# Second attention of a small vision tower: 68-column block-diagonal weights, dense head rows, sums from a column of ones

## The reference, cut to what matters

```
dist = softmax(mean(x @ Wr + br, axis=1))          # one row of 16 per image
idx = sort(top_k(dist, 4))
Qs, Ks, Vs = the 4 chosen heads of x @ Wq + bq, x @ Wk + bk, x @ Wv + bv    # 64 features each
score = softmax(Qs Ks^T / 8)                       # 17 x 17 per image and head
O = score Vs                                       # 17 x 64 per image and head
return h + O.reshape(b, s, 256) @ Wo + bo
```

## Time and profile before

| | us |
|---|---|
| median of three runs | 391.5 |
| profiled execution | 390.81 |
| its span | 389.0 |
| TensorE busy | 314.6 (81%) |
| VectorE busy | 257.0 (66%) |
| ScalarE busy | 203.2 (52%) |
| GpSimd busy | 169.3 (44%) |
| TensorE's mean granted clock | 0.851 of full speed |

### The profile page before, as it was taken

How to read it: one execution, slowest core, us unless ns; L and a number is a source line. 1 busy time by engine, 2 the same in 40 slices (tenths; PEclk the granted TensorE clock), 3 DMA queues, 4 the chain that set the end, 5 groups by cost and what they waited for, 6 DMA issues and landing times.

```text
span 389.0 us, 14942 instructions
## 1 busy us (share of the span) xinstructions
PE 314.6 (81%) x6334; PEld 253.9 (65%) x6334; DVE 257.0 (66%) x546; ACT 203.2 (52%) x463; POOL 169.3 (44%) x193
## 2 busy tenths in 40 slices
PE   1999999888977888785897468998889698585787
PEld 0897768535855565554795258888789687483366
DVE  2355446455578888887696776797878678462365
ACT  1023323465877777742488037777777566352320
POOL 4755000004266666642055074576657656563200
PEclk9999999999975555555698559999999999679989
DMA  7997810003500000000000068999998899824714
GB/s 206 373 424 246 248 79 0 0 0 127 199 4 5 4 3 6 3 5 3 3 2 1 0 211 266 287 289 288 258 284 272 241 286 276 249 51 97 229 54 178
DMA packets 52275, 55.97 MB, mean 144 GB/s; under 512 B 25296, under 2 KB 49008, under 8 KB 51696
## 3 DMA queue, kind: packets, MB, share of 16 engines
q1 hardware_dynamic: 51632, 52.78, 43.1%
q0 software_dynamic: 576, 2.23, 1.8%
HBM read 45.04 MB, written 9.96 MB: 141 GB/s over the span
## 4 chain that ended last, share of the span: by engine, by line
PE 37%; SPq 23%; DVE 14%; issue 10%; DMA 6%; ACT 6%; POOL 4%; POOLq 0%; ACTq 0%; DVEq 0%
SPq L457 21%; PE ps L1366 11%; PE ps L1389 5%; PE ps L1520 4%; POOL r L527 4%; DVE r L1022 4%; PE ps L1727 3%; PE ps L1449 2%; DVE rs L1032 2%; PE ps L1404 2%; PE ps L1471 2%; DVE mx L1007 2%; DMA ring<-wsplit 2%; DMA r<-in_x 2%; DMA r<-padded_rows,idx 2%
## 5 line engine op out<-in xcount | busy, mean ns | idle before, releaser
L520 POOL TENSOR_TENSOR r<-r,cst 128x1088 f32<-128x1088 f32 x16 | 33.0, 2062 | 61.6 <-DVE ring L958 58.7
L1366 PE MATMUL ps<-r 128*128 128x256 f32 x192 | 45.8, 395 | 8.6 <-DMA r<-in_x 8.6
L1366 PEld LDWEIGHTS ps<-r 128*128 128x128 f32 x192 | 37.7, 199 | 15.6 <-issue 10.5
L805 ACT ACTIVATE r<-ps 128x504 f16<-128x504 f32 (+1 forms) x50 | 31.9, 664 | 27.9 <-PE ps L1571 27.5
L1594 PE MATMUL ps<-r,ring 128*128 128x68 f16 x840 | 34.6, 201 | 12.2 <-DMA ring<-wsplit 11.3
L1471 PE MATMUL ps<-r 17*32 17x34 f32 x2048 | 30.5, 242 | 16.1 <-DVE r L1022 11.2
L1471 PEld LDWEIGHTS ps<-r 17*32 17x32 f32 x2048 | 27.3, 142 | 24.1 <-DVE r L1022 18.3
L1594 PEld LDWEIGHTS ps<-r,ring 128*128 128x128 f16 x840 | 32.1, 101 | 16.5 <-DMA ring<-wsplit 13.2
L733 ACT ACTIVATE r<-r,cst 128x136 f32<-128x136 f32 x128 | 39.9, 401 | 0.0
L609 POOL TENSOR_TENSOR r<-r,quad 128x476 f16<-128x476 f16 x38 | 37.4, 1010 | 0.6
L527 POOL TENSOR_TENSOR r<-r,rinv 128x544 f32<-128x544 f32 x16 | 18.3, 1142 | 35.3 <-DVE rinv L1036 35.3
(11 more groups left out here) (170 smaller groups left out, 696.2 us busy)
## 6 DMA issues: line engine op xcount, KB each, us to landing
ring<-wsplit SPq DMA_DIRECT2D x140, 192.0 KB, 3.3
r<-in_x SPq DMA_DIRECT2D x3, 1536.0 KB, 15.9
padded_rows<-r SPq DMA_DIRECT2D x9, 448.0 KB, 5.2
r<-in_w SPq DMA_DIRECT2D x4, 768.0 KB, 7.5
wsplit<-ring SPq DMA_DIRECT2D x1, 3072.0 KB, 11.6
r<-in_x SPq DMA_DIRECT2D x4, 384.0 KB, 8.9
h<-in_pos SPq DMA_DIRECT2D x1, 1536.0 KB, 12.1
out<-h SPq DMA_DIRECT2D x3, 512.0 KB, 2.9
```

Of the source, the lines that this page charges most:

```text
L520: pool.tensor_tensor(free(kx[:, u % 2, 0, :], (ROWH, UI), (NTOK, HH), (1, NTOK)), free(kr[:, 0, UI * NTOK * u:], (NTOK, UI), (0, HH), (1, ...
L1366: mm = pe.matmul(bank((n - 1) % 2, 0, D), xT[:, c, k, i * P:(i + 1) * P], tokw[:, k, :], start=k == 0, stop=k == PKT - 1)
```

## The change

Three things change together, all in the second attention.

1. The blocks of `bd` stand at columns 17 j, 68 columns to a tile. There are no gaps to zero, the matmul of `weigh2` has 68 output partitions, and the four pairs' rows come out one after another.
2. `o2` takes 68 partitions. The store goes to `pair_rows`, where a pair has 17 rows: 68 partitions x 14 tiles x 64 floats instead of 128 x 14 x 64. Its pieces are still 256 bytes. The gather's index is the pair itself, not 32 times the pair, and it still reads 4,352 bytes per image and slot.
3. A column of ones stands beside the 64 columns of values (`VCOL = 66`, the last one unused; the low part has a zero there). The matmul takes 65 columns, and the last one gives the sum of the exponents. `total` and `inverse` go; `head_out` first takes the reciprocal of 68 x 7 sums out of PSUM and then multiplies.

```diff
-PITCH = QROW * HD2
+PITCH = NTOK * HD2
+VCOL = HD2 + 2
-        bd = r1[:, _bd:_bd + 2 * GU * P].bitcast(F16).rearrange("p (u x g n) -> p u x g n", u=2, x=2, g=GU)
+        bd = r1[:, _bd:_bd + 2 * GU * TCOL].bitcast(F16).rearrange("p (u x g n) -> p u x g n", u=2, x=2, g=GU)
...
-            return bass.AP(padded_rows.tensor, (v * PU + IPG * lo) * PITCH, [(HD2, P), (IPG * PITCH, n), (1, HD2)])
+            return bass.AP(pair_rows.tensor, (v * PU + IPG * lo) * PITCH, [(HD2, TCOL), (IPG * PITCH, n), (1, HD2)])
...
-                sp.dma_start(rows_of(v), o2[:, v % 2]).then_inc(o2_stored[v % 2], 16)
+                sp.dma_start(rows_of(v), o2[0:TCOL, v % 2]).then_inc(o2_stored[v % 2], 16)
...
-            for u in range(2):
-                pool.memset(free(bd[:, u, 0, 0, NTOK:], *gaps), 0.0).then_inc(bd_clear, 1)
+            for x in range(2):
+                pool.memset(free(v2[:, 0, x, 0, HD2:], (2 * GU * VCOL, 2), (VCOL, GU), (1, 1)), 1.0 - x).then_inc(ones_set, 1)
...
-                pool.tensor_tensor(free(bd[:, v % 2, x, GR * r, :], (P, GR), (QROW, IPG), (1, NTOK)),
+                pool.tensor_tensor(free(bd[:, v % 2, x, GR * r, :], (TCOL, GR), (NTOK, IPG), (1, NTOK)),
...
-                nc.scalar.activation(free(v2[:, v % 2, 0, GR * r, :], (1, GR * HD2)), bank(4, 0, GR * HD2), ACT.Copy,
+                nc.scalar.activation(v2[:, v % 2, 0, GR * r:GR * r + GR, 0:HD2], free(bank(4), (HD2, GR), (1, HD2)), ACT.Copy,
...
-            dve.tensor_scalar(idx[:, :], at_slot, float(QROW), None, ALU.mult).then_inc(idx_ready, 1)
+            dve.tensor_copy(idx[:, :], at_slot).then_inc(idx_ready, 1)
...
-            def total(v):
-                if v >= 2:
-                    dve.wait_ge(rinv2_ready, v - 1)
-                dve.tensor_reduce(rs[:, v % 2, 0:GU], p2[:, v % 2, :, 0:NTOK], AX_X, ALU.add).then_inc(rs2_ready, 1)
-
-            def inverse(v):
-                dve.wait_ge(rs2_ready, v + 1)
-                if v >= 2:
-                    dve.wait_ge(o2_ready, 2 * (v - 1))
-                dve.reciprocal(rinv[:, v % 2, 0:GU], rs[:, v % 2, 0:GU]).then_inc(rinv2_ready, 1)
-
             def head_out(v, r):
-                dve.wait_ge(pv2_done, 2 * v + r + 1)
-                dve.wait_ge(rinv2_ready, v + 1)
+                at = 2 * v + r
+                dve.wait_ge(pv2_done, at + 1)
                 if v >= 2:
                     dve.wait_ge(o2_stored[v % 2], v // 2 * 16)
-                dve.tensor_tensor(o2[:, v % 2, GR * r:GR * r + GR, :], free(bank(weigh_bank(v, r)), (HD2, GR), (1, HD2)),
-                                  free(rinv[:, v % 2, GR * r:], (1, GR), (0, HD2)), ALU.mult).then_inc(o2_ready, 1)
+                dve.reciprocal(rinv[0:TCOL, r, 0:GR], free(bank(weigh_bank(v, r), HD2)[0:TCOL], (VCOL, GR)))\
+                    .then_inc(rinv2_ready, 1)
+                dve.wait_ge(rinv2_ready, at + 1)
+                dve.tensor_tensor(o2[0:TCOL, v % 2, GR * r:GR * r + GR, :],
+                                  free(bank(weigh_bank(v, r))[0:TCOL], (VCOL, GR), (1, HD2)),
+                                  free(rinv[0:TCOL, r, :], (1, GR), (0, HD2)), ALU.mult).then_inc(o2_ready, 1)
...
-                        mm = pe.matmul(bank(weigh_bank(v, r), HD2 * i, HD2 * i + HD2), bd[:, v % 2, b, g, :], v2[:, v % 2, x, g, :],
-                                       start=m == 0, stop=m == 2)
+                        mm = pe.matmul(bank(weigh_bank(v, r), VCOL * i, VCOL * i + HD2 + 1)[0:TCOL], bd[:, v % 2, b, g, :],
+                                       v2[:, v % 2, x, g, 0:HD2 + 1], start=m == 0, stop=m == 2)
```

More of the change, by code:

```diff
@@ L100, in build @@
         _bd = 2 * _half
-        bd = r1[:, _bd:_bd + 2 * GU * P].bitcast(F16).rearrange("p (u x g n) -> p u x g n", u=2, x=2, g=GU)
-        _og = _bd + 2 * GU * P
+        bd = r1[:, _bd:_bd + 2 * GU * TCOL].bitcast(F16).rearrange("p (u x g n) -> p u x g n", u=2, x=2, g=GU)
+        _og = _bd + 2 * GU * TCOL
         og = r1[:, _og:_og + NSLOT * NTOK * HD2].rearrange("p (s n) -> p s n", s=NSLOT)
@@ L116, in build @@
         latk = r2[:, 5632:6144]
[L117 to L120, removed]
+        _o2 = 2 * GU * VCOL
+        v2 = r2[:, 0:_o2].bitcast(F16).rearrange("p (u x g d) -> p u x g d", u=2, x=2, g=GU)
+        o2 = r2[:, _o2:_o2 + 1792].rearrange("p (u g d) -> p u g d", u=2, g=GU)
+        _p2 = _o2 + 1792
+        p2 = r2[:, _p2:_p2 + 896].rearrange("p (u g q) -> p u g q", u=2, g=GU)
+        p2T = r2[:, _p2 + 896:_p2 + 1792].rearrange("p (u g q) -> p u g q", u=2, g=GU)
         r3 = sb("r3", 2 * 2 * B * NTOK + B * QROW)
@@ L218, in build @@
         bo_ready = sem("bo_ready")
-        bd_clear = sem("bd_clear")
+        ones_set = sem("ones_set")
         picked = sem("picked")
@@ L304, in build @@
         exp2_done = sem("exp2_done")
-        rs2_ready = sem("rs2_ready")
         rinv2_ready = sem("rinv2_ready")
@@ L472, in _ @@
                 sp.wait_ge(o2_ready, 2 * (NV - 1) + lo // GR + 1)
-                sp.dma_start(rows_of(NV - 1, lo, GR), o2[:, (NV - 1) % 2, lo:lo + GR])\
+                sp.dma_start(rows_of(NV - 1, lo, GR), o2[0:TCOL, (NV - 1) % 2, lo:lo + GR])\
                     .then_inc(o2_stored[(NV - 1) % 2], 16)
@@ L574, in keys_twice @@
                     pool.wait_ge(xg_clear, 4)
-                    pool.wait_ge(bd_clear, 2)
+                    pool.wait_ge(ones_set, 2)
                 elif v <= 1 and (v, r) != (1, 1):
@@ L646, in _ @@
             for s in range(NSLOT):
-                pool.indirect_dma_start(og[:, s, :], None, padded_rows,
+                pool.indirect_dma_start(og[:, s, :], None, pair_rows,
                                         bass.IndirectOffsetOnAxis(ap=idx[:, s:s + 1], axis=0))\
@@ L840, in pick @@
                     act.wait_ge(p2T_ready, v - 1)
-                    act.wait_ge(rs2_ready, v - 1)
                 for j in range(IPG):
@@ L888, in _ @@
                 for i in range(IPG):
-                    nc.scalar.activation(free(bd[:, (NV - 1) % 2, x, GR, QROW * i:], (P, GR), (1, NTOK)),
+                    nc.scalar.activation(free(bd[:, (NV - 1) % 2, x, GR, NTOK * i:], (TCOL, GR), (1, NTOK)),
                                          free(p2Tx[:, (NV - 1) % 2, x, GR], (QROW, GR), (1, NTOK)), ACT.Copy,
@@ L1226, in v_low @@
                 dve.scalar_tensor_tensor(
-                    out=free(v2[:, v % 2, 1, GR * r, :], (1, GR * HD2)), in0=bank(4, 0, GR * HD2),
-                    scalar=1 / (XS * WS), in1=free(v2[:, v % 2, 0, GR * r, :], (1, GR * HD2)),
+                    out=v2[:, v % 2, 1, GR * r:GR * r + GR, 0:HD2], in0=free(bank(4), (HD2, GR), (1, HD2)),
+                    scalar=1 / (XS * WS), in1=v2[:, v % 2, 0, GR * r:GR * r + GR, 0:HD2],
                     op0=ALU.mult, op1=ALU.subtract).then_inc(v2_low, 1)
@@ L1291, in _ @@
                     head_out(v - 2, 1)
-                if v >= 1:
-                    total(v - 1)
                 v_low(v, 1)
-                if v >= 1:
-                    inverse(v - 1)
                 if 1 <= v < NV - 2:
@@ L1306, in _ @@
             v_low(NV - 1, 0)
-            total(NV - 2)
             head_out(NV - 3, 1)
             soft_in(NV - 1)
-            inverse(NV - 2)
             turn(NV - 1)
@@ L1313, in _ @@
             v_low(NV - 1, 1)
-            total(NV - 1)
             head_out(NV - 2, 1)
-            inverse(NV - 1)
             head_out(NV - 1, 0)
@@ L1636, in weigh2 @@
                 if v < 2:
-                    pe.wait_ge(bd_clear, 2)
+                    pe.wait_ge(ones_set, 2)
                 pe.wait_ge(v2_low, 2 * v + r + 1)
```

1 line of the change is left out of this document (removed).

## The result

The changed kernel takes 401.3 us (median of four runs) against 391.9 us for the kernel before in the same comparison, ratio **1.025, 95% interval 1.020 to 1.030**: slower, as forecast, by 9.4 us; the forecast of 404 us lies 12.5 us above the median of 391.5. Its profiled execution took 402.75 us with a span of 400.9, 11.9 us over that of before; it is the slowest of its four runs, which is part of that difference.

What follows compares the result with a forecast made beforehand. It took the DMA engines, and SyncE stalling on them, to bound the second attention. From the profiled 390.8 us, 9.1 for rounds, 3.9 for the end and 0.5 for reciprocals gave 404 us; range 388 to 414.

Steps and rivals of the forecast that it cites:

- Number of engines: Stores of the second attention: completions follow rows in equal shares, so 68 rows run as 17 on each of 4 engines.
- 16-engine rival: Stores spread over all 16 engines in unequal shares: rounds of 10.7 us, 382 us in all; chance 0.16.
- The rounds: Six rounds with a store in the second attention: 13.5 us each, 1.5 us more, 9.1 us in all.
- The weights: Weights' transfers in each round of the second attention: 8.27 us of work on each of 16 engines.
- The store: Store of a round: 238 pieces at 17.9 ns, 4.3 us on each of 4 engines, against 2.0 us now.
- The surplus: Time of a round over its DMA work: 1.7 us before; a 7% idle share assumed after the change.
- SyncE as the carrier: SyncE's queue in the rounds stalls behind stores, so the 4 engines set the pace of the weights' transfers.
- the rival in which the weights give way: Four engines, but weights packets run faster: rounds hold at 12.0 us, 393 to 395 us; chance 0.12.
- The floor of a round: Rounds of the second attention: TensorE's work some 9.5 us, SyncE's own pace 9.7 us.
- The end: Last full store and halves on 4 engines, ahead of the gathers: done at 361.2 against 357.3, 3.9 us later.
- The gaps and the first rounds: Smaller clears put GpSimd 3 us earlier at 231 us; gain 0, covered by SyncE's 9.7 us per round.
- Loads of 68 columns: TensorE's loads in the second attention: 0 taken, up to 62 ns more each at the upper end.

Runs made afterwards that it cites:

- the first execution: The changed kernel's profiled execution in its first comparison with the kernel before: 402.75 us, the slowest of its four runs.
- the second one: The changed kernel run once more, unaltered, beside the kernels with 20 rows for a pair: median 399.5 us, ratio 1.025 to the kernel before.

## Why the prediction was right, and where its sizes were off

- **Number of engines.** The step from 3088 completions to equal shares, 17 rows on each of four engines, was right. The changed kernel posts four completions per store. 17, 34, 64, 80 and 124 rows give by the same count 1, 2, 16, 16 and 4, and for the extra transfer of 70 rows 14 are left: in each case the largest number up to 16 that divides the rows. So the Trainium skill's rule (DMA: Bandwidth & Descriptors, "Why a DMA increments its semaphore by 16 and not by 1") holds in all cases here. The 16-engine rival at 382 us didn't come, and where one transfer of 64 or 80 rows brought a store onto 16 engines, it gave 384.5 to 387, with rounds of 11.2 to 11.5 us instead of the rival's 10.7.
- **The rounds.** Forecast 13.5 us and 9.1 us in all, measured 13.41 and 8.6. That the sum came so close is partly luck: none of its three terms was right, and their errors offset each other. *The weights* were put at 8.27 us of work. But that is the work of a stretch of 9.25 us with 1911 packets, and a whole round has 14 x (128 + 16) = 2016, which makes 8.7 us. *The store* was priced at the 17.9 ns that its packets last. With 16 engines at work that is nearly the pace too. Where only stores run at the end of the kernel before, from 350.89 to 359 us in fortieths, they move about 218 GB/s, 18.8 ns for each piece on each engine:

```profile
GB/s 0 0 0 0 71 247 221 218 215 221 215 218 217 220 174 23 83 119 250 145 240 220 206 222 227 225 229 163 35 18 5 0 0 0 0 0 0 0 0 0
```

But four engines that work off a store of 68 rows move 72 GB/s and one moves 18, which is 256 / 18 = 14.2 ns per piece. The packets last as long as before and overlap: from 268.2 to 269.8 us of the changed kernel's trace 447 of them fill 31.4% of 16 engines, 18.0 ns each, and four engines are only 25% of 16. So the store's work is 3.4 us on each and not 4.3. *The surplus* of a round over this work is then 13.41 - 8.7 - 3.4 = 1.3 us, where I took 0.9; in the kernel before it is 11.97 - 8.7 - 2.1 = 1.2, and not 1.7. It stayed as it was, and the round grew by what the store's work grew.
- **SyncE as the carrier.** That the stalls of SyncE pass the store on to the weights was right, and the rounds with 238 pieces on one engine show that it is enough for one engine to be behind. Of the rival in which the weights give way nothing was seen: no round with 238 or more pieces on an engine was as short as that of before. (The 12% with which that rival holds the round at 12.0 us doesn't follow from the terms either; with the idle share of 7% it takes 17%.)
- **The floor of a round.** The prediction put TensorE's work at 9.5 us and SyncE's own pace at 9.7. Without stores a round takes 10.7 us, with TensorE busy for 9.9 of it. This left the forecast alone, since rounds of 13.4 us lie above it; but it means that the 16-engine rival's 10.7 us had no room left for a store.
- **The end.** Forecast +3.9 us from the last full store to TensorE's going on; measured 371.46 - 362.90 = 8.6 us against 357.52 - 350.89 = 6.6, +1.9. This term was mis-sized by the same price: 1.8 + 476 x 0.0142 = 8.6 us is what was measured, with 0.0179 it would be 10.3. What came ahead of it, +1.7 us in the first execution (the last weights landed in 4.88 us there, 3.73 before), didn't come again in the second one, where they landed in 3.87. There the last full store starts at 356.30 us, lands in 5.05 again, and the first gather is issued at 365.56 (SyncE's queue and GpSimd's timeline):

```profile
342.04 14.51 SPq L462 DMA_DIRECT2D pair_rows<-r  x3
```

```profile
365.56 1.15 POOL L648 DMA_INDIRECT r<-pair_rows,idx  x1 [8.05 <-issue]
```

That is 9.3 us from store to gathers, as in the first execution, against 7.3 before. From the last weights on it is 23.5 us, against 26.3 in the first execution and 22.6 before. So 8.6 us in the rounds and 1.9 us behind the last full store are what both executions show, 10.5 us, and the interval of the ratio, 7.6 to 11.8 us, agrees. From the last weights to the last full store it is 17.0 us in the first execution, 14.3 in the second and 15.3 before, and the change's share in that stays open.
- **VectorE.** Two reciprocals in the chain, 0.17 and 0.21 us, as costed. The run with the column of ones alone bounds the whole part at -0.05% to +1.3%; it doesn't settle more.
- **The gaps and the first rounds.** No gain from 3 us less of GpSimd: 39.5 us for the first 56 transfers against 38.9. Right. The kernels with 20 rows for a pair took longer there, 41.1, 40.6 and (128 columns) 42.5 us, and SyncE waited 1.2 and 3.5 us for TensorE in the first and the last of them. They clear for 1.1 and 3.4 us more on GpSimd, but so did the kernel before, by 3.2 us, with 38.9; the cause isn't shown. They are faster in spite of it.
- **Loads of 68 columns.** 0 was taken at ends of 0 and 62 ns; 117 against 100 ns for a load (means) and 3 ns in pace are measured. The Trainium skill's statement (TensorE: Matmul & The Clock Gate, "Weight-path perf modes — Fast Weight Load (FWL) and DoubleRow") agrees in direction with these traces, as the load of 128 columns is the faster one. The Trainium skill's figure of columns / 1.2 (the same page, "LDWEIGHTS (loading the stationary operand)"), an estimated 57 ns at a pace, does not fit them: 21 matmuls in 0.86 us leave, less the 0.2 us of one matmul by itself and over 20 steps, a pace of about 33 ns.

What isn't settled: why one engine with 238 pieces costs less than four do (ratio 1.008 against 1.025), and whether SyncE is held by a limit on transfers under way or on pieces; no run changed one without the other. Nor is the line of the table a price of a piece that holds everywhere. At the end, with stores alone, 64 rows on 16 engines move only 154 GB/s, 26.6 ns for a piece on each engine, where 128 rows on 16 engines take 18.8 and 68 rows on four 14.2. Why is open.

## What to carry to other kernels

Before a transfer's rows are cut down, count the engines that its outermost number leaves: 128 to 68 rows halved the pieces and doubled them on the engines that still worked, and 124 rows were worse than 128. Where other transfers need all engines and one queue carries them, as here, the fullest engine sets most of the pace of all. A few rows of padding up to a multiple of 16 (80 for 68) cost less than a number that leaves four engines, and less than a second small transfer. And a saved transfer is worth no more than the next floor, here 10.7 us per round of computing.

## What the runs showed that I had not expected

- Small packets overlap on an engine when few engines work: 18 ns long by their share of busy time, 14.2 ns apart by their rate (18 GB/s on one engine, 72 on four). With 16 engines and 128 rows they come 18.8 ns apart.
- A second transfer with 56 pieces in all, behind one of 64 rows, costs 0.8 us per round (12.12 against 11.36), as much as some 65 more pieces per engine at 11.8 ns.
- A group of 21 matmuls takes 0.97 us with loads of 80 columns, 0.86 with 68 and 0.80 with 128.
